# First image of an attention stage: the transposed softmax is copied before the input is shifted, powers cut by image, sign products moved

## The chip, the cores and the metric

The kernel runs on one core of a Trainium2 chip. The time is device time in microseconds of one execution of the whole program. A core has five engines, each with its own queue of instructions, that meet only at semaphores: the matrix engine (PE, with its weight loads PEld), VectorE (DVE), ScalarE (ACT), GpSimd (POOL) and SyncE (SP), which here issues the loads and stores.

## The reference

The input `x` is 4 images of 512 channels of 16 x 16 positions. Four blocks follow, each with a residual around a group norm (32 groups) and a branch:

```
x = x + _L0_conv_ref(_gn(x), ...)   # attention
x = x + _L1_conv_ref(_gn(x), ...)   # scan over columns, forward and back, with a PReLU
x = x + _L2_conv_ref(_gn(x), ...)   # attention
x = x + _L3_conv_ref(_gn(x), ...)   # scan over rows, forward and back, with a relu

def _L0_conv_ref(x, w1, b1, w2, b2, w3, b3, alpha):
    e1 = jax.nn.relu(jnp.einsum('dc,ncp->ndp', w1, xf) + b1[None, :, None])
    e2 = jax.nn.relu(jnp.einsum('dc,ncp->ndp', w2, xf) + b2[None, :, None])
    assembly = jax.nn.relu(jnp.einsum('oc,ncp->nop', w3, xf) + b3[None, :, None])
    scores = jnp.einsum('ndi,ndj->nij', e1, e2)
    attn = jax.nn.softmax(scores, axis=-1)
    out = jnp.einsum('ncj,nij->nci', xf, attn)
    y = alpha[0] * out + assembly
```

## The kernel before

Channels lie on the 128 partitions, in K = 4 blocks, so a block of an image is a tile of 128 x 256. All is float32. The stages run one after another: norm and attention 0, norm and scan 1, norm and attention 2, norm and scan 3. An attention runs over the four images; each engine has its own loop over them (`images`, with the first and the last image written apart). The order of work on an engine is the order of its code; semaphores do the rest.

One image of an attention goes like this. ScalarE writes the normalised image `xn` (VectorE does it for the first image). The matrix engine makes the two embeddings (L400), ScalarE their relu. Then come the scores (L419), VectorE's row maximum `mx` (L789) and its negative `nmx`, ScalarE's exponential, and VectorE's scaling of `prob` by the sum and by alpha (L803). The matrix engine transposes `prob` in two halves (L438). ScalarE copies the first half to `probT` (L593) and VectorE the second (L827). With both copies there (`pt_copied`) the matrix engine makes the output products from `xT` and `probT` (L453), which VectorE scales and adds to the residual `rx` (L837), followed by the statistics of the result for the next norm (L679). The relu branch of 16 products (L388) is spread between these steps to fill the matrix engine: its last three stand between the transposes and the output products. ScalarE writes its relu as `rel` (L597).

The residual `rx` is the relu branch with a sign (that of the next stage's PReLU) plus `shifted`, the input with a per-channel shift and the sign: `shifted_input` (L779), then `add_residual` (L818). In images 1 to 3 `shifted_input` stands at the image's beginning, ahead of the maximum. In the first image it stands behind the norm's second round.

The norm of stage 0 has two rounds: the first image alone, then images 1 to 3 together (`norm_rounds`). For each round VectorE delivers `gvar` and `gneg`, and GpSimd (`inverse_std`) raises `gvar` to -0.5 (`rstd`, L1054), multiplies to `nmr` (L1059) and from that makes `shift` (L1070). ScalarE's `normalise_next` waits for the second `nmr` (`norm[l].done`). GpSimd then multiplies stage 2's weights by the sign (`signed_weights`, L1133): `w12` in four products of 128 x 128 and `w3` in four of 128 x 512. Its next work is the norm of stage 1.

Of the kernel before, what the change touches and what calls it, by code (L numbers as in the profile page):

```python
# [23 lines left out]
K = C // P  # L24
# [7 lines left out]
NC = N * K  # L32
# [96 lines left out]
def preact_stack(nc, a):  # L129
    with ExitStack() as ctx:  # L130
# [3 lines left out]
        def sem(name):  # L134
            return ctx.enter_context(nc.semaphore(name))
# [78 lines left out]
        s_shift = sem("shift_ready")  # L214
# [8 lines left out]
        s_signed12, s_signed3 = sem("w12_signed"), sem("w3_signed")  # L223
# [3 lines left out]
        norm = [NormSems(sem, l) for l in range(4)]  # L227
        att = {l: AttentionSems(sem, l) for l in (0, 2)}
# [11 lines left out]
        def image_in(l, n):  # L240
            if l == 0:
                return x0[:, n]

            return xw.rearrange("p n k (w h) -> p n k w h", h=T)[:, n]
# [14 lines left out]
        def norm_rounds(l):  # L259
            first = K if l in (0, 2) else NC - K  # L260
            return [(0, first), (first, NC)]

        by_vector = {0: 3, 2: 2}
# [289 lines left out]
        def _(act):  # L556
# [3 lines left out]
            def attention(l, b12, b3):  # L560
                s = att[l]

                def image(n, h, first=False, last=False):
                    act.wait_ge(s.e_mm, n + 1)
                    for rows in (slice(0, D), slice(D, 2 * D)):
                        nc.scalar.activation(e1[rows], bank[1][0:D, 0:POS], ACT.Relu,  # L566
                                             bias=par[0:D, b12:b12 + 1]).then_inc(s.e_ready, 1)
                        nc.scalar.activation(e2[rows], bank[1][D:2 * D, 0:POS], ACT.Relu,
                                             bias=par[D:2 * D, b12:b12 + 1]).then_inc(s.e_ready, 1)
                    act.wait_ge(s.nmx_ready, n + 1)  # L570
                    for ic in range(PC):
                        nc.scalar.activation(prob[:, ic], scores[:, ic * POS:(ic + 1) * POS], ACT.Exp,  # L572
                                             bias=nmx[:, ic:ic + 1], accum_out=rsum[:, ic:ic + 1])\
                            .then_inc(s.exp_done, 1)


                    def normalise_next():
                        act.wait_ge(norm[l].done, 2)
                        for k in range(K):
                            src, dst = image_in(l, n + 1)[:, k], xn[1 - h][:, k]  # L580
                            if l == 2:
                                dst = dst.rearrange("p (t j) -> p t j", t=T)
                            c = (n + 1) * K + k
                            nc.scalar.activation(dst, src, ACT.Identity, bias=nmr[:, bass.ds(c, 1)],
                                                 scale=rstd[:, bass.ds(c, 1)]).then_inc(s.xn_ready, 1)


                    for m in range(K):
                        if m == 0:
                            act.wait_ge(s.a_mm, n * 2 + 1)  # L590
                        if m == 2:
                            act.wait_ge(s.pt_mm, n * PC + 1)
                            nc.scalar.copy(by_rows(l, probT[:, 0]), in_order(l, bank[1][:, 0:POS])).then_inc(s.pt_copied, 1)  # L593
                            if not last and not first:
                                normalise_next()
                            act.wait_ge(s.a_mm, n * 2 + 2)
                        nc.scalar.activation(rel[:, m], bank[2 + m // 2][:, m % 2 * POS:(m % 2 + 1) * POS],  # L597
                                             ACT.Relu, bias=par[:, b3 + m:b3 + m + 1]).then_inc(s.r_ready, 1)
                    if first:
                        normalise_next()  # L600
                    if last:
                        scan_inputs(l + 1, 0, range(N - 1), 1)

                images(act, image)
# [64 lines left out]
        def _(dve):  # L669
# [98 lines left out]
            def attention(l, alpha):  # L768
                s = att[l]

                def image(n, h, first=False, last=False):


                    def shifted_input():
                        dve.wait_ge(s_shift, (1 if first else 2) + l)
                        for m in range(K):
                            moved = shift[:, bass.ds(n * K + m, 1)]
                            if l == 0:
                                nc.vector.tensor_scalar(shifted[:, m], x0[:, n, m], moved, sign[:, 0:1],  # L779
                                                        ALU.add, ALU.mult).then_inc(s.shifted, 1)  # L780
                            else:
                                nc.vector.tensor_scalar(in_order(l, shifted[:, m]), image_in(l, n)[:, m],
                                                        sign[:, 0:1], moved, ALU.mult, ALU.add)\
                                    .then_inc(s.shifted, 1)
# [22 lines left out]
                        set_variances(l, 1)  # L807
                    if first:
                        variances(l, 1)
                        shifted_input()  # L810
                    if last:
                        variances(l + 1, 0)

                    def add_residual(m):
                        dve.wait_ge(s.r_ready, n * K + m + 1)
                        dve.wait_ge(s.shifted, n * K + m + 1)
                        if l == 0:
                            nc.vector.scalar_tensor_tensor(rx[:, m], rel[:, m], sign[:, 0:1], shifted[:, m],  # L818
                                                           ALU.mult, ALU.add).then_inc(s.rx_done, 1)
                        else:  # L820
                            nc.vector.tensor_tensor(by_rows(l, rx[:, m]), in_order(l, rel[:, m]),
                                                    in_order(l, shifted[:, m]), ALU.add).then_inc(s.rx_done, 1)

                    add_residual(0)
                    add_residual(1)
                    dve.wait_ge(s.pt_mm, n * PC + 2)
                    nc.vector.tensor_copy(by_rows(l, probT[:, 1]), in_order(l, bank[0][:, 0:POS])).then_inc(s.pt_copied, 1)  # L827
                    for m in range(2, by_vector[l] if last else K):
                        add_residual(m)
                    for m in range(K):  # L830
                        dve.wait_ge(s.o_mm, n * K + m + 1)
# [4 lines left out]
                        o, r = (v.rearrange("p (t j) -> p t j", t=T) for v in (o_bank(m), rx[:, m]))  # L836
# [197 lines left out]
        def _(pool):  # L1034
# [11 lines left out]

            def inverse_std(l):
                s = norm[l]
                done = 0
                for r, (c0, c1) in enumerate(norm_rounds(l)):  # L1050
                    width = K // 2 if c1 - c0 == K else c1 - c0
                    pool.wait_ge(s.gvar, r + 1)
                    for c in range(c0, c1, width):
                        nc.gpsimd.tensor_tensor(rstd[:, c:c + width], gvar[:, c:c + width], mhalf[:, c:c + width],  # L1054
                                                ALU.pow).then_inc(s.rstd, 1)
                        done += 1
                    pool.wait_ge(s.neg, r + 1)
                    pool.wait_ge(s.rstd, done)
                    nc.gpsimd.tensor_tensor(nmr[:, c0:c1], gneg[:, c0:c1], rstd[:, c0:c1], ALU.mult)\  # L1059
                        .then_inc(s.done, 1)  # L1060
                    if l in scan:
                        input_bias(l, r, c0, c1)
                        if r == 0:
                            last_residuals(l - 1)
                    if l in att:

                        pool.wait_ge(s_small, 32)
                        pool.wait_ge(s.done, r + 1)
                        alpha = par[:, AL_0:AL_0 + 1] if l == 0 else signal[:, 1:2]
                        nc.gpsimd.tensor_tensor(shift[:, c0:c1], nmr[:, c0:c1], alpha.to_broadcast([P, c1 - c0]),  # L1070
                                                ALU.mult).then_inc(s_shift, 1)
# [56 lines left out]
            def signed_weights():  # L1128
                pool.wait_ge(s_sign, 1)
                for w, loaded, done in ((w12[2], s_w12[2], s_signed12), (w3[2], s_w3[2], s_signed3)):  # L1130
                    pool.wait_ge(loaded, 16)
                    for k in range(K):
                        nc.gpsimd.tensor_tensor(w[:, k], w[:, k], sign[:, 0:1].to_broadcast([P, w.shape[2]]), ALU.mult)\  # L1133
                            .then_inc(done, 1)

# [56 lines left out]
```

## Time and profile before

| | |
|---|---|
| median of 3 runs | 262.6 us (262.56 to 262.82) |
| the profiled execution | 262.56 us, span 260.8 us |
| matrix engine busy | 253.3 us, 97% of the span |
| VectorE busy | 176.5 us, 68% |
| ScalarE busy | 95.6 us, 37% |
| GpSimd busy | 69.1 us, 27% |

The span is that of the trace, from the first to the last instruction; the execution's time has 1.76 us around it. Each float32 matmul stands in the trace as two records, so "x6" are three products. Consecutive records of an engine overlap a little: the distance of two starts is the pace, the duration of one is longer.

### The profile page before, as it was taken

The numbers are of one execution on the slowest core, as the hardware profiler recorded it, in microseconds if no ns is written. First come the engines' busy times: TensorE is split into PE (matmuls) and PEld (weight loads), VectorE is DVE, ScalarE is ACT, GpSimd is POOL, SyncE is SP. The second block draws the span as 40 slices with busy tenths as digits, with TensorE's granted clock in tenths as the row PEclk, the third lists the DMA queues.
The fourth block names the chain that finished last, engine by engine and source line by source line (L and its number), as shares of the span: only waits on it lengthen the run. The fifth ranks groups of instructions, "written<-read, shape, count | busy, mean of one in ns | idle before, by whom it ended". The sixth has DMA issues, their size and how long they took to land.

```text
span 260.8 us, 11036 instructions
## 1 busy us (share of the span) xinstructions
PE 253.3 (97%) x4485; PEld 221.2 (85%) x4488; DVE 176.5 (68%) x667; ACT 95.6 (37%) x229; POOL 69.1 (27%) x106
## 2 busy tenths in 40 slices
PE   8997999999989999999999999999999999999995
PEld 2776887878679999999997788878886999999995
DVE  2789866675777777777788785575858655545553
ACT  2144554545763333433326553637258200000000
POOL 0207500006332222333332040000053433334342
PEclk9999999999999999999999999999999999999999
DMA  6999000000000000000000000000000000011222
GB/s 210 403 379 400 21 0 0 4 0 0 0 6 0 0 0 0 1 0 0 0 0 4 0 0 3 1 0 0 1 3 0 3 0 0 0 35 66 70 71 80
DMA packets 5199, 11.47 MB, mean 44 GB/s; under 512 B 704, under 2 KB 3264, under 8 KB 4672
## 3 DMA queue, kind: packets, MB, share of 16 engines
q1 hardware_dynamic: 4896, 10.76, 11.1%
q10 hardware_dynamic: 288, 0.52, 0.6%
q8 instruction: 8, 0.13, 0.2%
q14 instruction: 7, 0.06, 0.1%
HBM read 9.19 MB, written 2.10 MB: 43 GB/s over the span
## 4 chain that ended last, share of the span: by engine, by line
PE 91%; DVE 5%; issue 1%; POOL 1%; ACT 0%; POOLq 0%; DVEq 0%; ACTq 0%
PE banks L491 46%; PE banks L388 20%; PE banks L453 11%; PE banks L400 5%; PE banks L331 4%; PE banks L419 2%; PE banks L438 1%; PE banks L474 1%; POOL rstd L1054 1%; DVE mx L789 1%; PE banks L355 1%; DVE st L679 1%; ACT inb L613 0%; PE banks L366 0%; DVE xn L765 0%
## 5 line engine op out<-in xcount | busy, mean ns | idle before, releaser
L491 PE MATMUL banks<-state,wc 128*64 128x64 f32 x3840 | 121.8, 224 | 1.3 <-DVE state L925 1.2
L491 PEld LDWEIGHTS banks<-state,wc 128*64 128x64 f32 x3840 | 117.1, 138 | 6.3 <-ACT banks L628 1.3
L388 PE MATMUL banks<-xn,w 128*128 128x256 f32 x256 | 61.0, 384 | 0.0
L388 PEld LDWEIGHTS banks<-xn,w 128*128 128x128 f32 x256 | 47.1, 190 | 7.2 <-issue 1.7
L903 DVE SCALAR_TENSOR_TENSOR state<-banks,negb,inb 128x64 f32<-128x64 f32 x116 | 29.2, 281 | 24.1 <-PE banks L491 24.0
L1054 POOL TENSOR_TENSOR rstd<-gvar,mhalf 128x2 f32<-128x2 f32 (+1 forms) x12 | 15.2, 1278 | 104.4 <-DVE gvar L754 100.4
L920 DVE SCALAR_TENSOR_TENSOR sloped<-banks,par,share 128x64 f32<-128x64 f32 x116 | 27.5, 280 | 15.1 <-PE banks L491 14.6
L453 PE MATMUL banks<-probT,xT 128*128 128x256 f32 x128 | 29.0, 380 | 1.4 <-DVE probT L827 1.4
L453 PEld LDWEIGHTS banks<-probT,xT 128*128 128x128 f32 x128 | 24.2, 190 | 5.0 <-issue 1.8
L925 DVE SCALAR_TENSOR_TENSOR state<-sloped,bent,banks 128x64 f32<-128x64 f32 x112 | 26.0, 275 | 0.0
L628 ACT COPY banks<-inb 128x256 f32 (+1 forms) x29 | 10.9, 376 | 37.1 <-DVE state L925 35.0
L566 ACT ACTIVATE e<-banks,par 64x256 f32<-64x256 f32 x16 | 7.5, 468 | 30.9 <-PE banks L400 30.7
L1119 POOL TENSOR_TENSOR xw<-xw,state 128x256 f32 (+1 forms) x15 | 11.1, 739 | 21.7 <-DVE state L925 21.7
L400 PE MATMUL banks<-xn,w 128*128 128x256 f32 x64 | 15.3, 381 | 0.4 <-DVE xn L765 0.4
L331 PE MATMUL banks<-zeros 128*128 128x512 bf16 x47 | 14.2, 440 | 1.4 <-DVE zeros L1020 1.2
L1119 POOL TENSOR_TENSOR xh<-xh,state 128x256 f32 (+1 forms) x15 | 10.9, 729 | 17.1 <-DVE state L903 17.1
L629 ACT ACTIVATE share<-inb,oma 128x256 f32 (+1 forms) x30 | 15.1, 505 | 0.0
L597 ACT ACTIVATE rel<-banks,par 128x256 f32<-128x256 f32 x32 | 13.3, 470 | 4.6 <-PE banks L388 4.6
L400 PEld LDWEIGHTS banks<-xn,w 128*128 128x128 f32 x64 | 12.0, 190 | 2.9 <-issue 1.4
L1113 POOL TENSOR_TENSOR inb<-state,signb 128x256 f32 x14 | 8.6, 612 | 19.4 <-DVE state L925 19.4
L1113 POOL TENSOR_TENSOR inb<-state,par 128x256 f32 x14 | 8.6, 614 | 16.1 <-DVE state L903 16.1
L572 ACT ACTIVATE prob<-banks,nmx 128x256 f32<-128x256 f32 x16 | 7.4, 469 | 14.2 <-DVE nmx L792 14.2
(112 smaller groups left out, 220.5 us busy)
## 6 DMA issues: line engine op xcount, KB each, us to landing
w<-in_w SPq DMA_DIRECT2D x2, 1024.0 KB, 12.1
xT<-in_xT SPq DMA_DIRECT2D x4, 512.0 KB, 12.2
wc<-in_wc SPq DMA_DIRECT2D x2, 1024.0 KB, 17.1
result<-xh SPq DMA_DIRECT2D x15, 128.0 KB, 1.8
x<-in_x SPq DMA_DIRECT2D x3, 512.0 KB, 8.5
x<-in_x ACTq DMA_DIRECT2D x1, 256.0 KB, 4.4
x<-in_x SPq DMA_DIRECT2D x1, 256.0 KB, 4.2
w<-in_w ACTq DMA_DIRECT2D x1, 256.0 KB, 4.9
```

The source lines that it names most:

```text
L331: nc.tensor.matmul(bank[b], zeros[:, 0:P], zeros[:], start=True, stop=True)
L388: mm = nc.tensor.matmul(bank[2 + m // 2][:, m % 2 * POS:(m % 2 + 1) * POS], w3[l][:, k, m * P:(m + 1) * P], xn_s[:, k], start=(k == 0), st ...
L400: mm = nc.tensor.matmul(bank[1][:, 0:POS], w12[l][:, k], xn[h][:, k], start=(k == 0), stop=(k == K - 1))
L453: mm = nc.tensor.matmul(o_bank(m), by_position[:, jc, m * P:(m + 1) * P], probT[:, jc], start=(jc == 0), stop=(jc == PC - 1))
L491: mm = nc.tensor.matmul(bank[K * h + m][c:c + TILE, 0:COLS], wc[l][:, k, m * P + c:m * P + c + TILE], state[:, h, k], start=first and not ...
L629: nc.scalar.activation(share[:, h], inb[:, t], ACT.Identity, scale=oma[:, 0:1]).then_inc(s.share, 1)
L903: nc.vector.scalar_tensor_tensor(new_state(q, h, k), like_new(q, product(k, h)), negb[:, k:k + 1], like_new(q, inb[:, t, k]), ALU.max, ALU ...
L920: nc.vector.scalar_tensor_tensor(sloped[:, k], summed(q, k, h), par[:, PA_1:PA_1 + 1], share[:, h, k], ALU.mult, ALU.add).then_inc(s.slope ...
L925: nc.vector.scalar_tensor_tensor(new_state(q, h, k), like_new(q, sloped[:, k]), bent[:, k:k + 1], like_new(q, summed(q, k, h)), ALU.add, A ...
L1054: nc.gpsimd.tensor_tensor(rstd[:, c:c + width], gvar[:, c:c + width], mhalf[:, c:c + width], ALU.pow).then_inc(s.rstd, 1)
L1113: nc.gpsimd.tensor_tensor(inb[:, t], state[:, 1 - h], bias, ALU.add).then_inc(s.taken, 1)
L1119: nc.gpsimd.tensor_tensor(xr[:, t], xr[:, t], by_image(state[:, h]), ALU.add).then_inc(s.taken, 1)
```

## The change

Four things are different, all of them in stage 0, the first attention; line numbers of the kernel after are 5 to 14 higher. In the first image VectorE's copy of the transposed softmax stands ahead of `shifted_input` and of all residuals. GpSimd's second round of powers is cut in two pieces, the columns of image 1 and those of images 2 and 3, each with its `nmr` and `shift`; the thresholds of those who wait for them are adapted. Each of the sign products waits for an output of the first attention: `w12` for the first output of image 0, two products of `w3` for the first output of image 1, two for that of image 2.

```diff
+        def power_rounds(l):
+            rounds = [(r, c0, c1) for r, (c0, c1) in enumerate(norm_rounds(l))]
+            return rounds if l else [rounds[0], (1, K, 2 * K), (1, 2 * K, NC)]
...
                     def normalise_next():
-                        act.wait_ge(norm[l].done, 2)
+                        act.wait_ge(norm[l].done, 2 if first or l else 3)
...
                     def shifted_input():
-                        dve.wait_ge(s_shift, (1 if first else 2) + l)
+                        dve.wait_ge(s_shift, (1 if first else 2 if l else 3) + (3 if l else 0))
...
                     if first:
                         variances(l, 1)
-                        shifted_input()
+                        if l == 2:
+                            shifted_input()
...
-                    add_residual(0)
-                    add_residual(1)
+
+                    late = first and l == 0
+                    early = 0 if late else 2
+                    for m in range(early):
+                        add_residual(m)
                     dve.wait_ge(s.pt_mm, n * PC + 2)
                     nc.vector.tensor_copy(by_rows(l, probT[:, 1]), in_order(l, bank[0][:, 0:POS])).then_inc(s.pt_copied, 1)
-                    for m in range(2, by_vector[l] if last else K):
+                    if late:
+                        shifted_input()
+                    for m in range(early, by_vector[l] if last else K):
                         add_residual(m)
...
-                done = 0
-                for r, (c0, c1) in enumerate(norm_rounds(l)):
-                    width = K // 2 if c1 - c0 == K else c1 - c0
+                done = pieces = 0
+                for r, c0, c1 in power_rounds(l):
+                    width = K // 2 if c1 - c0 == K and (l, r) != (0, 1) else c1 - c0
...
-                        pool.wait_ge(s.done, r + 1)
+                        pieces += 1
+                        pool.wait_ge(s.done, pieces)
...
                     for k in range(K):
+
+                        pool.wait_ge(att[0].x_done, 1 if done is s_signed12 else K * (1 + k // 2) + 1)
                         nc.gpsimd.tensor_tensor(w[:, k], w[:, k], sign[:, 0:1].to_broadcast([P, w.shape[2]]), ALU.mult)\
```

On VectorE, in the first image of the first attention, from the second round's variance to the first output, the kernel before has this order:

```order
L754 TENSOR_REDUCE gvar<-banks 128x12
L779 TENSOR_SCALAR shifted<-x,shift,sign 128x256 x4
L818 SCALAR_TENSOR_TENSOR rx<-rel,sign,shifted 128x256 x2
L827 COPY probT<-banks 128x256
L818 SCALAR_TENSOR_TENSOR rx<-rel,sign,shifted 128x256 x2
L837 SCALAR_TENSOR_TENSOR xw<-banks,rstd,rx 128x256
```

And the kernel after, in the same place:

```order
L759 TENSOR_REDUCE gvar<-banks 128x12
L836 COPY probT<-banks 128x256
L784 TENSOR_SCALAR shifted<-x,shift,sign 128x256 x4
L824 SCALAR_TENSOR_TENSOR rx<-rel,sign,shifted 128x256 x4
L848 SCALAR_TENSOR_TENSOR xw<-banks,rstd,rx 128x256
```

The copy has moved ahead of four shifts and two residuals; no instruction is added or taken away here.

On GpSimd, from the end of the first round to the norm of stage 1, the kernel before has this order (`w_2` stands for both weights of stage 2; in brackets the semaphores):

```order
L1054 TENSOR_TENSOR rstd<-gvar,mhalf 128x12 [waits gvar_ready0]
L1059 TENSOR_TENSOR nmr<-gneg,rstd 128x12 [waits rstd_ready0,mean_negated0]
L1070 TENSOR_TENSOR shift<-nmr,par 128x12 [waits norm_ready0,small_loaded]
L1133 TENSOR_TENSOR w_2<-w_2,sign 128x128 [waits w12_loaded2,sign_set]
L1133 TENSOR_TENSOR w_2<-w_2,sign 128x128 x3
L1133 TENSOR_TENSOR w_2<-w_2,sign 128x512 [waits w3_loaded2]
L1133 TENSOR_TENSOR w_2<-w_2,sign 128x512 x3
```

And the kernel after:

```order
L1065 TENSOR_TENSOR rstd<-gvar,mhalf 128x4 [waits gvar_ready0]
L1070 TENSOR_TENSOR nmr<-gneg,rstd 128x4 [waits rstd_ready0,mean_negated0]
L1082 TENSOR_TENSOR shift<-nmr,par 128x4 [waits norm_ready0,small_loaded]
L1065 TENSOR_TENSOR rstd<-gvar,mhalf 128x8 [waits gvar_ready0]
L1070 TENSOR_TENSOR nmr<-gneg,rstd 128x8 [waits rstd_ready0,mean_negated0]
L1082 TENSOR_TENSOR shift<-nmr,par 128x8 [waits norm_ready0,small_loaded]
L1147 TENSOR_TENSOR w_2<-w_2,sign 128x128 [waits x_done0,w12_loaded2,sign_set]
L1147 TENSOR_TENSOR w_2<-w_2,sign 128x128 [waits x_done0] x3
L1147 TENSOR_TENSOR w_2<-w_2,sign 128x512 [waits x_done0,w3_loaded2]
L1147 TENSOR_TENSOR w_2<-w_2,sign 128x512 [waits x_done0] x3
```

Three instructions more stand ahead of the sign products, and each sign product waits for `x_done` of the first attention.

## Rows read from the trace of the kernel before

**Rows 1.** The page: busy time by engine, and the granted clock in 40 slices

```profile
PE 253.3 (97%) x4485; PEld 221.2 (85%) x4488; DVE 176.5 (68%) x667; ACT 95.6 (37%) x229; POOL 69.1 (27%) x106
...
PEclk9999999999999999999999999999999999999999
```

**Rows 2.** Timeline of the matrix engine, image 0: start, duration, line, in brackets idle before

```profile
18.11 0.60 PE L438 MATMUL banks<-ident,prob 128*128 128x128 f32 x4
...
18.93 1.54 PE L388 MATMUL banks<-xn,w 128*128 128x256 f32 x6
21.87 3.69 PE L453 MATMUL banks<-probT,xT 128*128 128x256 f32 x16 [1.40 <-DVE probT L827]
25.39 1.89 PE L400 MATMUL banks<-xn,w 128*128 128x256 f32 x8
```

**Rows 3.** The chain that ended last, images 0 and 1: start, its share of time

```profile
21.87 3.69 PE banks L453 x16
25.56 1.73 PE banks L400 x8
...
35.46 3.45 PE banks L453 x16
```

**Rows 4.** Timeline of VectorE, images 0 and 1

```profile
19.12 0.18 DVE L754 TENSOR_REDUCE gvar<-banks 128x12 f32<-128x24 f32 x1 [0.41 <-PE banks L355]
19.22 1.37 DVE L779 TENSOR_SCALAR shifted<-x,shift,sign 128x256 f32<-128x256 f32 x4
20.52 0.87 DVE L818 SCALAR_TENSOR_TENSOR rx<-rel,sign,shifted 128x256 f32<-128x256 f32 x2
21.31 0.41 DVE L827 COPY probT<-banks 128x256 f32<-128x256 f32 x1
21.64 0.87 DVE L818 SCALAR_TENSOR_TENSOR rx<-rel,sign,shifted 128x256 f32<-128x256 f32 x2
23.01 0.48 DVE L837 SCALAR_TENSOR_TENSOR xw<-banks,rstd,rx 128x256 f32<-128x256 f32 x1 [0.50 <-PE banks L453]
...
26.46 3.56 DVE L779 TENSOR_SCALAR shifted<-x,shift,sign 128x256 f32<-128x256 f32 x4
30.12 0.69 DVE L789 TENSOR_REDUCE mx<-banks 128x2 f32<-128x512 f32 x1
...
37.51 0.48 DVE L837 SCALAR_TENSOR_TENSOR xw<-banks,rstd,rx 128x256 f32<-128x256 f32 x1
```

**Rows 5.** SyncE's issue of the transposed input, and the loads' times to landing

```profile
4.97 2.42 SPq L309 DMA_DIRECT2D xT<-in_xT  x4
...
DMA to landing us min/median/max: 11.2/12.2/13.0
```

**Rows 6.** Timeline of GpSimd and ScalarE, image 0

```profile
19.39 2.37 POOL L1054 TENSOR_TENSOR rstd<-gvar,mhalf 128x12 f32<-128x12 f32 x1 [9.08 <-DVE gvar L754]
20.51 0.84 ACT L597 ACTIVATE rel<-banks,par 128x256 f32<-128x256 f32 x2 [1.61 <-PE banks L388]
21.90 0.29 POOL L1059 TENSOR_TENSOR nmr<-gneg,rstd 128x12 f32<-128x12 f32 x1
22.22 2.08 ACT L584 ACTIVATE xn<-x,nmr,rstd 128x256 f32<-128x256 f32 x4 [0.87 <-POOL nmr L1059]
23.27 1.47 POOL L1133 TENSOR_TENSOR w<-w,sign 128x128 f32<-128x128 f32 x4 [0.70 <-DMA w<-in_w]
25.70 4.17 POOL L1133 TENSOR_TENSOR w<-w,sign 128x512 f32<-128x512 f32 x4 [0.95 <-DMA w<-in_w]
```

**Rows 7.** Timeline of VectorE, image 2

```profile
40.91 1.37 DVE L779 TENSOR_SCALAR shifted<-x,shift,sign 128x256 f32<-128x256 f32 x4
43.48 0.69 DVE L789 TENSOR_REDUCE mx<-banks 128x2 f32<-128x512 f32 x1 [1.20 <-PE banks L419]
```

**Rows 8.** GpSimd's powers by shape: count, busy us, mean ns

```profile
L1054 POOL TENSOR_TENSOR rstd<-gvar,mhalf 128x12 f32<-128x12 f32 x4 | 9.6, 2401 | 84.5 <-DVE gvar L754 84.5
L1054 POOL TENSOR_TENSOR rstd<-gvar,mhalf 128x2 f32<-128x2 f32 x8 | 5.6, 717 | 19.9 <-DVE gvar L754 15.9 <-DVE gvar L751 4.0
```

## The prediction

> **What bounds the kernel now.** I read the page first. The matrix engine is busy 97% of a 260.8 us span and its granted clock stands at full in all 40 slices [rows 1]. So time can only be won where that engine stands still, and a saving on any other engine is worth what it takes out of such a gap. The second view is the timeline of the matrix engine from 18 to 27 us, inside the first image of the first attention. The reader is to see one gap: the relu branch's last three products (six records) start at 18.93 and end at 20.47, and the output products L453 start only at 21.87, after 1.40 us idle, released by the vector engine's copy of the transposed softmax, L827 [rows 2]. In the chain that ended last the same 16 records take 3.69 us in this image, behind the gap, and 3.45 us in the next image, where they follow the relu branch without one [rows 3]. The difference, 0.24 us, is what the pipeline pays to start again.
>
> The third view is the vector engine in the same stretch [rows 4]. The transposes that the copy needs are done at 18.11 + 0.60 = 18.71 [rows 2]. From then on the vector engine does gvar (19.12), four shifts of the input (19.22), two residuals (20.52), and only at 21.31 the copy. The copy was possible some two microseconds before.
>
> **The change, part by part.**
>
> *The copy moves ahead of the four shifts and the first two residuals.* The instruction ahead of it is gvar, which starts at 19.12 and takes 0.18, so the copy starts between 19.22 (where the first shift started) and 19.33. With its 0.41 it ends by 19.75 [rows 4]. Before, it ended at 21.72 and the products started at 21.87, 0.15 later; now that hand-over is done by 19.90. In the chain's shape of a gapless image the products join on to a relu branch ending at 20.47. So the copy has some 0.3 to 0.5 us to spare, and the stop is gone whole: 20.47 + 3.45 = 23.92 instead of 25.56 [rows 3]. Gain: 1.40 + 0.24 = **1.64 us**. The lower bound of this term is 1.40, if the restart's 0.24 stays in part for another reason.
>
> *What else L453 waits for.* It also needs the ScalarE half of the copy, which in this order is before the branch's third unit and unchanged, and the transposed input of image 0. The four loads of that are issued from 4.97 on over 2.42 us and land 11.2 to 13.0 us later [rows 5]. The first can't be later than 4.97 + 13.0 = 18.0, or 18.6 counted from the end of its own issue. Both are ahead of 20.2. Cost nothing; if the last landing were meant, 7.39 + 13.0 = 20.4 still costs at most 0.2.
>
> *The shifts and residuals behind the copy.* Pitches are read from starts: four shifts 20.52 - 19.22 = 1.30; two residuals 21.31 - 20.52 = 0.79; the copy 21.64 - 21.31 = 0.33 [rows 4]. The shifts start at 19.33 + 0.33 = 19.66, the residuals at 20.96, and four of them end at 20.96 + 1.58 = 22.54. Their inputs are there: ScalarE's last two relus run from 20.51 to 21.35 [rows 6], and the third residual is reached at 21.75. Output m of the products comes 1.14 us after their start (23.01 - 21.87), so with a start at about 20.23 (21.87 - 1.64) the first is there at 21.37 and the vector engine, at 22.54, is now the later one. It is still 0.47 earlier than today's 23.01. The four pairs of output and statistics take 26.46 - 23.01 = 3.45 and end at 25.99, after which it does the four shifts of image 1, 1.30, to about 27.3 [rows 4].
>
> The next instruction on the vector engine that the matrix engine waits for is the row maximum of image 1. It started at 30.12 [rows 4], so it is due at 30.12 - 1.64 = 28.48. That leaves 28.48 - 27.3 = **1.2 us of slack**, the same as the 1.20 us that the maximum of image 2 waits for the matrix engine today [rows 7]. So no wait takes the place of the one removed, as long as the shifts of image 1 run at their own pace.
>
> *The sign products, moved.* Today the shifts of image 1 do not run at their own pace: they take 3.56 us against 1.37 in image 2 [rows 4, 7], and GpSimd works on the four wide sign products from 25.70 to 29.87 in just that time [rows 6]. The cost, 2.19 us, is hidden today, since the shifts end at 30.02 and the maximum starts at 30.12. With the matrix engine 1.64 ahead it would not be hidden: 25.99 + 3.56 = 29.55 against 28.48, a loss of 1.07. The edit moves the wide products to the fifth and ninth output, two in image 1 and two in image 2. Two take 4.17 / 2 = 2.09 us, and start 0.5 us into a stretch of 3.4 us (37.51 to 40.91) of outputs from PSUM and statistics [rows 4, 7], so they end about 0.8 us before the next shifts. That such pairs are not slowed by a sign product is shown by the narrow ones: they run from 23.27 to 24.74 [rows 6] in the pairs of image 0, and the four pairs take 3.45 there and 3.40 in image 1. Price: nothing. If the cover fails, two products cost the shifts at most 2.19 / 2 = 1.1 us, within the 1.20 of slack of that image. Nothing else is queued behind them on GpSimd but the power of the next stage's norm, which needs the statistics of image 3.
>
> *The powers, cut in pieces.* Two columns take 0.72 us and twelve 2.40 [rows 8]: (2.40 - 0.72) / 10 = 0.168 a column. No row shows 4 or 8 columns. By that line they are 1.05 and 1.73; the bounds are 0.72 and 2.40 for each. The power of image 1 then runs 19.39 to 20.44, its scaled mean (0.29, with a gap of 0.14 ahead as today [rows 6]) to 20.87, and ScalarE, busy until 21.35, normalises image 1 from about 21.3 instead of 22.22. Its four blocks take 2.08 and are ready from 21.8 to 23.4. The matrix engine wants the first at 25.39 - 1.64 = 23.75 [rows 2] and the last three quarters of L400's 1.73 us [rows 3] later, at 25.05. At the bound of 2.40 ScalarE starts at 22.22 as today, the first block is ready near 22.75 and the last at 24.30: nothing either. So this edit is worth 0 here; its cover is 1.0 us for the first part.
> The second power starts near 21.2 and ends near 22.9; with its two small ones GpSimd reaches the narrow sign products at about 23.7, where their load is there already (23.27 today), and they end near 25.2, ahead of the shifts at 25.99. At 2.40 for both powers they run to some 27.3, into those shifts, and cost at most their 1.47 us less the slack of 1.2, that is 0.3.
>
> **Sum.** The profiled execution took 262.56 us, with a span of 260.8; the median of the three runs is 262.60. 262.56 - 1.64 = 260.92, span 259.2; against the median **260.96 us**. Behind image 1 the program is a chain of semaphores with nothing tied to absolute time but the loads, so the shift carries to the end.
>
> **A rule that speaks against it.** The row shows that the power of twelve columns (19.39 to 21.76) ran over four shifts and two residuals, which took 1.37 and 0.87 [rows 4, 6], for the shifts the same as in image 2 with GpSimd idle [rows 7]: a power does not hold the vector engine. The Trainium skill, "SBUF — State Buffer", section "SBUF: two separate sides", says that VectorE and GpSimd share a port pair as an exclusive lock, taken for a whole instruction, against a VectorE operation in a two-port mode or with two SBUF inputs. By it the new powers would hold shifts and residuals and the gain would be gone (second rival); by the row the sum stands as it is. The slow shifts under the wide sign products agree with the page, the power does not.
>
> **The rivals.**
> 1. *The vector engine becomes the bound in image 1*, since products still meet its shifts. For it: the 3.56 us. Against: the new waits. If the whole 1.07 above is lost the gain is 0.57, 262.03.
> 2. *Same.* GpSimd's powers hold the vector engine: 1.05 + 1.73 = 2.78 us lost between 19.7 and 23, less 1.2 of slack, is 1.58 of 1.64: 262.5. Against it stands the power over today's shifts. An output product that waits for its load instead of the copy would end there too; the landing times exclude it.
> 3. *Slower.* The same holding applied to everything GpSimd does in image 0: the powers 2.78, the narrow products 1.47 and four small ones of 0.29 make 5.4 us; less 1.2 and less 1.64 this is 2.6 over today: 265.2. It decides from 1.2 + 1.64 = 2.84 us of holding on, of which the traces show none in this stretch.
>
> **How the numbers follow.** The main case has 0.88, the first rival 0.05 (half of it still beyond 0.2% faster), the second 0.04, the third 0.03. 0.2%, 0.53 us, is about what a measurement tells from no change; faster means below 262.07. The main case runs from 260.96 - 0.1 for the runs' spread, and less 0.2 for what may come with it, to 260.96 + 0.24 (restart not won) + 0.3 (narrow products late), with 0.1 of spread: 260.65 to 261.6. It holds a little over 8 in 10. Faster 0.91, same 0.06, slower 0.03.
>
> **What the new profile should show.** The copy starts at 19.2 to 19.4 and the matrix engine has no gap over 0.2 us between 17 and 54 us. L453 of image 0 starts near 20.2 and its 16 records end near 23.9. The first output starts at 22.5, released by the residual and no longer by the products. The shifts of image 1 take 1.4, not 3.6, end near 27.4, and the maximum waits about 1.2 for the matrix engine and starts at 28.5. Every later stage is 1.6 earlier. I am wrong if that maximum waits for nothing, or if the wide products in images 1 and 2 stretch the outputs beyond 3.5 us for four.

## The result, and the profile after

The kernel after takes 261.01 us (median of 4 runs, 260.88 to 261.14) against 262.59 for the kernel before; the ratio is 0.9938, with a 95% interval of 0.9921 to 0.9955. The span of the profiled execution is 259.2 us. The forecast was 260.96, with a range of 260.65 to 261.6.

The timeline of the matrix engine of the kernel after, in image 0 (it answers to [rows 2]; the lines are 5 higher):

```profile
18.22 0.60 PE L443 MATMUL banks<-ident,prob 128*128 128x128 f32 x4
...
19.04 1.54 PE L393 MATMUL banks<-xn,w 128*128 128x256 f32 x6
20.42 3.62 PE L458 MATMUL banks<-probT,xT 128*128 128x256 f32 x16
23.87 1.89 PE L405 MATMUL banks<-xn,w 128*128 128x256 f32 x8
```

The output products now have no idle time ahead of them and start while the relu branch's last record drains (19.04 + 1.54 = 20.58). The chain of the kernel after says the same (it answers to [rows 3]):

```profile
19.20 1.38 PE banks L393 x6
20.58 3.45 PE banks L458 x16
24.03 1.73 PE banks L405 x8
```

From the relu branch's start to the embeddings' there were 25.39 - 18.93 = 6.46 us, and there are 23.87 - 19.04 = 4.83: 1.63 less. This execution reached the place 0.11 us later than that of before (19.04 against 18.93), which the change doesn't touch; the spans differ by 1.6.

The timeline of VectorE of the kernel after (it answers to [rows 4] and [rows 7]):

```profile
19.34 0.41 DVE L836 COPY probT<-banks 128x256 f32<-128x256 f32 x1
19.66 1.37 DVE L784 TENSOR_SCALAR shifted<-x,shift,sign 128x256 f32<-128x256 f32 x4
20.95 1.66 DVE L824 SCALAR_TENSOR_TENSOR rx<-rel,sign,shifted 128x256 f32<-128x256 f32 x4
22.54 0.47 DVE L848 SCALAR_TENSOR_TENSOR xw<-banks,rstd,rx 128x256 f32<-128x256 f32 x1
...
25.93 1.37 DVE L784 TENSOR_SCALAR shifted<-x,shift,sign 128x256 f32<-128x256 f32 x4
28.60 0.69 DVE L794 TENSOR_REDUCE mx<-banks 128x2 f32<-128x512 f32 x1 [1.31 <-PE banks L424]
```

The first output has no wait for the products any more, the shifts of image 1 take 1.37 us instead of 3.56, and the maximum waits 1.31 us for the matrix engine. GpSimd and ScalarE (they answer to [rows 6]; the last row shows two of the wide sign products, in image 1):

```profile
19.50 1.01 POOL L1065 TENSOR_TENSOR rstd<-gvar,mhalf 128x4 f32<-128x4 f32 x1 [9.07 <-DVE gvar L759]
...
20.99 0.50 POOL L1082 TENSOR_TENSOR shift<-nmr,par 128x4 f32<-128x4 f32 x1
21.35 2.07 ACT L589 ACTIVATE xn<-x,nmr,rstd 128x256 f32<-128x256 f32 x4
21.44 1.88 POOL L1065 TENSOR_TENSOR rstd<-gvar,mhalf 128x8 f32<-128x8 f32 x1
...
36.61 2.04 POOL L1147 TENSOR_TENSOR w<-w,sign 128x512 f32<-128x512 f32 x2 [11.17 <-DVE xw L848]
```

### The profile page after: what moved, and what is told of

It reads as the page before. It is cut to its first block, busy times and chain, and to the rows that moved or that the text cites. A ratio compares the mean times of both kernels' runs of the same rounds, so it can differ in the third digit from the quotient of the medians.

```text
span 259.2 us, 11042 instructions
## 1 busy us (share of the span) xinstructions
PE 253.0 (98%) x4485; PEld 221.4 (85%) x4488; DVE 174.1 (67%) x667; ACT 95.5 (37%) x229; POOL 70.0 (27%) x109
## 4 chain that ended last, share of the span: by engine, by line
PE 90%; DVE 5%; DMA 2%; POOL 1%; issue 1%; ACT 0%; POOLq 0%; DVEq 0%; ACTq 0%
PE banks L496 46%; PE banks L393 20%; PE banks L458 11%; PE banks L405 6%; PE banks L424 2%; DMA x<-in_x 2%; PE banks L336 1%; PE banks L443 1%; PE banks L479 1%; DVE st L684 1%; POOL rstd L1065 1%; DVE mx L794 1%; PE banks L360 1%; PE banks L371 0%; ACT inb L618 0%
## 5 line engine op out<-in xcount | busy, mean ns | idle before, releaser
L1065 POOL TENSOR_TENSOR rstd<-gvar,mhalf 128x2 f32<-128x2 f32 (+3 forms) x13 | 15.8, 1220 | 80.9 <-DVE gvar L759 76.9
```

## The experiments

Eight kernels ran, each 4 to 11 times beside the kernel before; the table gives medians. All but e1, which leaves two parts of the change out, differ from the kernel after by one edit.

| kernel | what it is | us | ratio to before, interval |
|---|---|---|---|
| e1 | only the copy moved | 261.66 | 0.9957, 0.9942 to 0.9971 |
| e2 | sign products not moved | 261.93 | 0.9968, 0.9959 to 0.9977 |
| e3 | powers not cut | 261.05 | 0.9941, 0.9928 to 0.9954 |
| e4 | VectorE's order of before | 262.77 | 1.0, 0.9992 to 1.0009 |
| e5 | two shifts ahead of the copy | 261.26 | 0.9947, 0.9933 to 0.9961 |
| e6 | four shifts ahead of the copy | 261.83 | 0.9972, 0.996 to 0.9984 |
| e7 | wide sign products on the shifts | 260.98 | 0.9942, 0.9929 to 0.9956 |
| e8 | variance products later | 259.86 | 0.9896, 0.9881 to 0.9911 |

The kernel before took 262.69 (23 runs) beside e1 to e4 and 262.6 (10 runs) beside e5 to e8.

### e1 and e2: the copy without the sign products' waits

e2 takes the wait out of the kernel after; e1 has the powers whole besides (the diff of e3).

```diff
-                        pool.wait_ge(att[0].x_done, 1 if done is s_signed12 else K * (1 + k // 2) + 1)
```

> The copy of the transposed softmax moved as in the change, the powers whole and the sign products unmoved, as before. My theory: the gap ahead of the output products of image 0 is gone, but the four wide sign products (25.7 to 29.9 us) now meet the shifts of image 1, which take about 3.5 us from 26.0 on and end near 29.5, where the maximum is due at 28.6: 0.9 to 1.1 us lost, so 261.9 to 262.1 us. Rival: the sign products don't matter for the time, the copy alone makes all of the gain: 261.0 us. Second rival: the power of twelve columns makes image 1's normalised blocks late: then a gap ahead of the embeddings L405 would show, none is expected.

> The kernel after, without the waits of the sign products for the outputs. GpSimd reaches the narrow ones at about 24.0 us as in the kernel after, the wide ones when their load is there, near 25.7. My theory: as e1, 261.9 to 262.1 us, shifts of image 1 about 3.5 us long, the maximum of image 1 starting about 1 us late (near 29.6) and waiting for nothing. Rival: 261.0 us.

Measured: 261.66 and 261.93 us. Timelines of e2, of VectorE, of GpSimd and of the matrix engine in image 1:

```profile
26.08 4.16 DVE L784 TENSOR_SCALAR shifted<-x,shift,sign 128x256 f32<-128x256 f32 x4
30.16 0.68 DVE L794 TENSOR_REDUCE mx<-banks 128x2 f32<-128x512 f32 x1
...
25.91 4.18 POOL L1146 TENSOR_TENSOR w<-w,sign 128x512 f32<-128x512 f32 x4 [0.31 <-DMA w<-in_w]
...
28.63 3.72 PE L393 MATMUL banks<-xn,w 128*128 128x256 f32 x16
33.13 0.66 PE L443 MATMUL banks<-ident,prob 128*128 128x128 f32 x4 [0.78 <-DVE prob L808]
```

The first gap is gone here too, and part of it comes back 12 us later: the shifts take 4.16 us, the maximum waits for nothing, and the matrix engine stands 0.78 us ahead of the transposes, waiting for the scaled softmax. The rival (the sign products don't matter) falls. It is the wide products that count: the narrow ones start at 23.97 in the kernel after and at 24.12 in e2, which reached the place 0.14 later, so their wait holds nothing back. The time of e2 landed where I put it, but by luck, since two errors cancel. The holding was larger than the 2.19 us I took from the kernel before: all four shifts now begin under a product, and each takes a product's time (4.18 for four) instead of its own 0.33. The price per microsecond was smaller. The transposes start 33.13 - 28.63 = 4.50 us after the relu records of image 1, in the kernel after 32.04 - 28.48 = 3.56, so 0.94 is lost; the maximum starts 1.53 after those records and 0.12 in the kernel after, so it was 1.41 late. The difference of 0.47 is a second slack that my sum did not have. In e1 the expected range was missed by 0.24, on the good side. Its runs lie between 261.03 and 262.17 and those of e2 between 261.4 and 262.37, both far wider than those of the kernel after. The start of the wide products hangs on the landing of their load in both kernels; that this makes the spread, or the difference between the two, is argued, not shown.

### e3: the powers not cut

```diff
-            return rounds if l else [rounds[0], (1, K, 2 * K), (1, 2 * K, NC)]
+            return rounds
...
```

(Not shown: the thresholds of those who wait for the pieces go back with it.)

> The kernel after, with the second round of powers whole again (one power of twelve columns). My theory: the scaled mean of image 1 comes near 22.3 us and ScalarE's first block near 22.8, before the 23.87 at which the embeddings start: nothing changes, 261.0 us within 0.15. Rival: the cut of the powers is what lets the embeddings follow without a gap; then L405 starts late and the time is above 261.5.

Measured: 261.05 us, no difference. GpSimd and ScalarE of e3:

```profile
21.82 0.78 POOL L1070 TENSOR_TENSOR nmr<-gneg,rstd 128x12 f32<-128x12 f32 x1
...
22.64 2.08 ACT L589 ACTIVATE xn<-x,nmr,rstd 128x256 f32<-128x256 f32 x4 [1.27 <-POOL nmr L1070]
```

The cut is worth nothing in time, but the margin is smaller than I had said: the scaled mean took 0.78 us instead of 0.29, and came 0.3 us later than expected. ScalarE ends at 24.72; the embeddings started at 23.78, and want the last block (by my estimate, after three quarters of their 1.73 us) 1.3 us later, at 25.08.

### e4: VectorE's order of before

```diff
                         variances(l, 1)
-                        if l == 2:
-                            shifted_input()
+                        shifted_input()
...
-                    late = first and l == 0
+                    late = False
```

> The kernel after, with VectorE's order of before (shifts and two residuals ahead of the copy); powers cut and sign products moved as in the change. My theory: the shifts of image 1 fall from 3.56 to 1.4 us, which brings nothing because they were hidden; the gap of 1.40 us is back: 262.6 us within 0.15. Rival: the moved sign products or the cut powers bring part of the gain by themselves: under 262.2.

Measured: 262.77 us, 0.02 beyond the range I gave, and the time of the kernel before, which took 262.69 beside it. The timelines of e4, of VectorE in image 1 and of the matrix engine in image 0:

```profile
26.52 1.36 DVE L784 TENSOR_SCALAR shifted<-x,shift,sign 128x256 f32<-128x256 f32 x4
30.18 0.69 DVE L794 TENSOR_REDUCE mx<-banks 128x2 f32<-128x512 f32 x1 [2.30 <-PE banks L424]
...
21.93 3.69 PE L458 MATMUL banks<-probT,xT 128*128 128x256 f32 x16 [1.40 <-DVE probT L835]
```

The shifts fall by 2.2 us and the whole of it turns into a wait of the maximum, 2.30 us. So without the copy's move there is no gain. With it alone (e1) there is 1.0 us of the 1.6, and the moved products keep the rest.

### e5 and e6: how much time the copy has

```diff
-                    def shifted_input():
+                    def shifted_input(ms=range(K)):
...
-                        for m in range(K):
+                        for m in ms:
...
+                    if late:
+                        shifted_input(range(2))
                     dve.wait_ge(s.pt_mm, n * PC + 2)
...
                     if late:
-                        shifted_input()
+                        shifted_input(range(2, K))
```

(e6 has 4 in place of 2.)

> The kernel after, with two of the four shifts of image 0 ahead of the copy. It starts 0.65 us later than in the kernel after (near 20.0) and is handed over near 20.55, where the relu branch ends at 20.58. My theory (the copy has 0.3 to 0.5 us to spare): 0.65 is just over that, the loss is 0.1 to 0.35, so 261.1 to 261.35 us. Rival: the copy's place matters only through the residuals behind ScalarE's relu, two shifts cost nothing: 261.0 us.

> The kernel after, with all four shifts of image 0 ahead of the copy, but no residual. The copy starts 1.30 us later, near 20.64, the products near 21.2. My theory: the loss is 1.30 less the spare time plus the restart, 0.8 to 1.05, so 261.8 to 262.05 us, and the matrix engine has a gap of about 0.6 us there. Rival: the gap is made by the two residuals and not by the shifts: 261.0 to 261.3 us.

Measured: 261.26 and 261.83 us, 0.25 and 0.82 over the kernel after, both in the range of my theory. Timelines, first of e5:

```profile
19.22 1.54 PE L393 MATMUL banks<-xn,w 128*128 128x256 f32 x6
...
20.16 0.42 DVE L838 COPY probT<-banks 128x256 f32<-128x256 f32 x1
...
20.72 3.69 PE L458 MATMUL banks<-probT,xT 128*128 128x256 f32 x16
```

and of e6:

```profile
19.12 1.54 PE L393 MATMUL banks<-xn,w 128*128 128x256 f32 x6
...
20.70 0.41 DVE L838 COPY probT<-banks 128x256 f32<-128x256 f32 x1
...
21.26 3.69 PE L458 MATMUL banks<-probT,xT 128*128 128x256 f32 x16 [0.60 <-DVE probT L838]
```

In e5, in e6 and before, the products start 0.56 us after the copy (20.72 - 20.16, 21.26 - 20.70, 21.87 - 21.31). Without a stop they start 1.38 after the relu branch (20.42 - 19.04, the kernel after), 0.16 before the branch's last record ends. So a copy that starts 1.38 - 0.56 = 0.82 after the branch costs nothing. It starts 0.30 after it in the kernel after, 0.94 in e5, 1.58 in e6 and 2.38 before. The times follow: over by 0.12, 0.76 and 1.56, and 0.25, 0.82 and 1.58 us of time (the last is before's 262.59). In rows, from the relu branch's start to the embeddings', the kernel after takes 4.83 us, e5 5.03 (24.25 - 19.22), e6 5.67 (24.79 - 19.12) and before 6.46: 0.20, 0.84 and 1.63 lost, each time 0.07 or 0.08 beyond the lateness. The products themselves then last 3.69 instead of 3.62. What the copy had to spare was 0.52 us. The rival of both, that only the residuals ahead of the copy count, falls: in e6 no residual stands there.

### e7: the wide sign products put on the shifts

```diff
-                        pool.wait_ge(att[0].x_done, 1 if done is s_signed12 else K * (1 + k // 2) + 1)
+                        pool.wait_ge(att[0].x_done, 1 if done is s_signed12 else K * (2 + k // 2))
```

> The kernel after, with the wide sign products placed on the shifts on purpose: two after the last output of image 1, two after that of image 2. My theory: each wide product holds the shifts for about 1.0 us, those of images 2 and 3 take 2.9 to 3.4 us instead of 1.37, the maximum starts 0 to 0.6 us late, and a second slack between the scaled softmax and the transposes (0.5 us in the traces) covers most of it: 261.0 to 261.3 us. Rival: GpSimd and VectorE share in proportion, shifts of 2.5 us, no loss at all. Second rival: each us of holding beyond the slack of 1.2 goes to the time: 261.6 us or more.

Measured: 260.98 us, as the kernel after (0.02 below my range). The timelines of e7 in image 2:

```profile
39.34 2.65 DVE L784 TENSOR_SCALAR shifted<-x,shift,sign 128x256 f32<-128x256 f32 x4
41.91 0.69 DVE L794 TENSOR_REDUCE mx<-banks 128x2 f32<-128x512 f32 x1
...
39.10 2.09 POOL L1147 TENSOR_TENSOR w<-w,sign 128x512 f32<-128x512 f32 x2 [13.71 <-DVE xw L848]
```

The shifts take 2.65 us (2.58 in image 3), 1.28 more than alone, and the slack of 1.2 us swallows it: the maximum starts 0.12 us behind the relu records, as in the kernel after. My 2.9 to 3.4 us was wrong: a product replaces a shift's own time, so two of them cost at most 2 x (1.04 - 0.33) = 1.4, and not two whole products.

The rival of a proportional slowing had 2.5 us as its number, and the totals don't exclude it: shifts at a third of their own pace under a product would give, as an estimate, 4.1 us in e2 and 2.6 in e7. The single shifts do. These are the four shifts of image 1 in the kernel before and the four of image 2 in e7 (shortest, median and longest, in ns):

```profile
L779 DVE TENSOR_SCALAR shifted<-x,shift,sign x4: 429/1124/1124, 26.5 to 28.9; 128x256 f32<-128x256 f32 x4
L784 DVE TENSOR_SCALAR shifted<-x,shift,sign x4: 399/680/1125, 39.3 to 41.6; 128x256 f32<-128x256 f32 x4
```

The first shift of the kernel before starts at 26.46, when the first wide product (25.70 to 26.74) has 0.28 us to go and the second follows at once. At a third of its pace it would have taken over 1 us; it took 0.43 and ended at 26.89, 0.15 behind the first product. In e2 the last shift ends at 30.24 and the last product at 30.09, 0.15 apart again. So a shift waits for the end of the product that runs, and gets its turn there although the next product has begun. How many wide products meet one image's shifts decides: two are free, four cost 0.9.

### e8: a better version

```diff
                     relu_branch(xn[h], 1, True, range(ahead, K))
+                    relu_branch(xn[h], 2, False, range(ahead))
                     if first and l == 2:
                         group_variances(l, 1)
                     if last:
                         group_variances(l + 1, 0)
-                    relu_branch(xn[h], 2, False)
+                    relu_branch(xn[h], 2, False, range(ahead, K))
...
+                    relu_branch(xn[h], 3, False, range(ahead, 2))
                     if first and l == 0:
                         group_variances(l, 1)
-                    relu_branch(xn[h], 3, True, range(ahead, K))
+                    relu_branch(xn[h], 3, True, range(2, K))
```

> The kernel after, with one change more on the matrix engine: the product that sums the variances (L360 of the kernel after), for which it stands still waiting for VectorE in the first and last image of both attentions, comes one relu product (0.43 us) later. In the traces it waits 0.1 to 0.2 us each time and pays a restart. My theory: about 0.2 us each at four places, 0.5 to 0.9 us in all, 260.1 to 260.5 us. Rival: in image 0 gvar, and with it the copy behind it, comes 0.2 us later and the copy has no time to spare, so part is given back there: 260.5 to 260.8 us.

Measured: 259.86 us (259.79 to 259.92), 1.15 us below the kernel after and 1% below the kernel before; more than either theory gave. The last image of the first attention, in the chain of the kernel after:

```profile
56.85 0.20 DVE vadd L748
57.04 0.04 issue
57.09 0.40 PE banks L360 x2
57.49 2.25 PE banks L393 x10
```

and in the chain of e8:

```profile
55.33 1.82 PE banks L393 x8
57.15 0.13 PE banks L360 x2
57.28 1.81 PE banks L393 x8
```

The variance product itself falls from 0.40 to 0.13 us of the chain, and VectorE's steps have left the chain. From the embeddings of image 1 to the start of the scan it is 72.35 - 24.03 = 48.32 us in the kernel after and 71.72 - 23.77 = 47.95 in e8. So what I had put at 0.2 us was 0.37 us at this place. It has three parts that the rows don't separate: the stop, the product's latency with nothing behind it, and the restart. The same reading of the two chains gives 0.23 in the first image of the first attention, 0.38 in the first image of the second and 0.37 in its last. In image 0 the product in e8 is issued 0.87 us after the transposes (19.07 - 18.20) instead of 0.58, and the copy starts at 19.50; the products follow the relu branch at 20.16, after 18.63 + 1.38 + 0.13 = 20.14, so the second theory's price was not paid in this place. It was paid in the first image of the second attention, where the shifts and two residuals still stand ahead of the copy. The chain has there, in the kernel after and then in e8:

```profile
151.77 3.45 PE banks L458 x16
150.75 3.68 PE banks L460 x16
```

In the timelines the copy starts 150.06 - 149.29 = 0.77 us behind the relu branch in e8 and 150.71 - 150.31 = 0.40 in the kernel after, and e8 gives back 0.23 us. Together this makes 0.37 + 0.23 + 0.38 + 0.37 - 0.23 = 1.12 of the 1.15 us. Moving that copy too was not tried.

## Why the prediction was right, point by point

**The gap and its worth.** 1.40 of idle time and 0.24 of restart make 1.64; the rows say 1.63, the medians 1.58. e4 shows that nothing of it comes without the copy's move. The step held, and its lower bound of 1.40 was not needed. The 0.24 has another make-up than "to start again" says: 0.16 is the overlap with the branch's last record, lost as soon as the products come late, and 0.07 a longer run of the products (3.69 against 3.62). e5 shows it: its timeline has no idle time ahead of the products, and they still cost 0.20.

**The copy's spare time.** "Some 0.3 to 0.5 us": e5 and e6 give 0.52.

**What else L453 waits for.** The landing of the transposed input was excluded by the bounds of [rows 5], and the products start without a stop.

**VectorE behind the copy.** Forecast for the first output 22.54, for the shifts of image 1 25.99 and for the maximum 28.48; measured 22.54, 25.93 and 28.60, in an execution 0.11 late at this place. The slack was 1.31 us for the 1.2 stated. The two signs of being wrong stayed away: the maximum does wait, and four pairs of output and statistics take 3.40 us in image 1 (39.39 - 35.99) and in image 2 (52.74 - 49.34).

**The sign products.** Right in what they would have cost (a loss of 1.07 was said for the kernel without their waits, e2 loses 0.92), but both of its terms were off, and that they cancel is luck: 2.8 us of holding instead of 2.19, and a second slack of 0.47 behind the maximum. The bound for two products on the shifts, 1.1 us, was too low as well: e7 has 1.28, and loses no time. The statement that pairs of output and statistics are not slowed by a sign product holds: the two products of image 1 (36.61 to 38.65) lie over pairs that take the same 3.40 us as in [rows 4, 7].

**The powers.** 1.01 for 4 columns (1.05 said; 1.25 and 1.26 in e4, e5 and e6) and 1.88 for 8 (1.73 said; 1.63 in e4). That their cut brings nothing is shown by e3. Its cover was overstated: for the first block 1.0 us was said and e3 leaves 0.6 (ready near 23.16, a quarter of ScalarE's 2.08 behind 22.64, and wanted at 23.78), for the last the prediction's times leave 0.75 and e3 leaves 0.36. The prediction let GpSimd run at its own pace behind the copy; its `shift` of four columns took 0.50 us and its second power 1.88, so the narrow products end at 25.44 instead of 25.2, still 0.5 ahead of the shifts.

**The rivals.** The second and third lived on GpSimd holding VectorE with its powers. In the kernel after the powers lie over the four shifts and four residuals, and these take 1.37 and 1.66: no holding. The narrow products of the third lie over outputs and statistics, which take 3.39 (25.93 - 22.54). The first rival exists, as e2, and the waits of the change are what keeps it away.

## What to carry to other kernels

A stop of the matrix engine is worth its idle time plus what the pipeline pays around it, which a row of the same group without a stop shows (3.69 against 3.45 here, and more for a lone product between others, as e8 showed). Before moving work ahead of something, write down how much later the waiting engine could take it: 0.82 us after the relu branch's start, here; inside that the order is free, outside it costs one for one, and some 0.08 us on top. And when a bound engine is moved forward, look at what was hidden behind its stop: a 2.2 us slowing that had been free would have taken over half of the gain.

## What the runs showed of the hardware

The holding goes both ways, and this I had not expected. A VectorE shift under a wide sign product waits for the end of the product (four shifts at 4.16 us, the products' 4.18, in e2), while outputs from PSUM and statistics don't (3.40 us for four pairs, with and without products over them). The other way, GpSimd's small operations wait for VectorE when it runs residuals, from `rel` and `shifted`. The scaled mean of 12 columns, 0.23 in the mean over the kernel before, took 0.78 us in e3 and 0.79 in e1. In e3 it starts inside the third of four residuals in a row and ends at 22.60, 0.07 behind the fourth. Before it took 0.29, from inside the third residual to 0.07 behind that one (22.18 against 22.11). Why it waits for one residual there and for two here is not shown. The power of 8 columns took 1.88 us where it began under four residuals in a row and 1.63 in e4, where two stood on each side of the copy. The Trainium skill, "SBUF — State Buffer", section "SBUF: two separate sides", has an exclusive lock for the whole instruction, also against a VectorE operation with two SBUF inputs. Shifts and small operations agree with it. The powers do not: one of 12 columns, 2.37 us long, lies over four shifts that lose nothing.
